# Attention B of a four-block transformer kernel: row maxima from four 32-row products at a time, the spread ahead of the second value block, the output copy behind the shift

## The reference

```
q = (x @ Wq.T).reshape(b, t, 8, 32)
kv_latent = x @ Wkv_down.T
k = (kv_latent @ Wk_up.T).reshape(b, t, 8, 32)
v = (kv_latent @ Wv_up.T).reshape(b, t, 8, 32)
scores = jnp.einsum('bqhd,bkhd->bhqk', q, k) * 32 ** -0.5
attn = jax.nn.softmax(scores, axis=-1)
out = jnp.einsum('bhqk,bkhd->bqhd', attn, v)
return out.reshape(b, t, 256) @ Wo.T
```

## Time and profile before

| | |
|---|---|
| median of three runs | 2250.07 us |
| the profiled execution's own time | 2249.5 us |
| its span | 2247.7 us |
| mean granted clock of TensorE | 0.981 of full speed |
| PE busy (share of the span) | 2099.7 us (93%) |
| DVE busy | 1919.2 us (85%) |
| ACT busy | 1734.8 us (77%) |
| POOL busy | 877.0 us (39%) |
| attention B's loop, first rate to last eviction | 1667.0 to 2116.2 us |

### The profile page before, as it was taken

How to read it: one execution, slowest core, us unless ns; L and a number is a source line. 1 busy time by engine, 2 the same in 40 slices (tenths; PEclk the granted TensorE clock), 3 DMA queues, 4 the chain that set the end, 5 groups by cost and what they waited for, 6 DMA issues and landing times. The chain is left out here.

```text
span 2247.7 us, 62135 instructions
## 1 busy us (share of the span) xinstructions
PE 2099.7 (93%) x24904; PEld 1428.6 (64%) x24904; DVE 1919.2 (85%) x2618; ACT 1734.8 (77%) x3070; POOL 877.0 (39%) x953
## 2 busy tenths in 40 slices
PE   6799999999999999999999999968779999999877
PEld 4467776777767777777777767754435656566644
DVE  6899999999999999999999999957678788887684
ACT  3789998999989999999999999942357777777532
POOL 4333323333223333333233233233017777777540
PEclk9999999999999999999999999988989999999988
DMA  3799999999999999999999999940141111111001
GB/s 102 119 197 195 195 196 185 195 193 193 193 194 197 194 197 195 191 197 189 198 194 191 194 192 194 197 83 1 35 137 31 30 31 33 34 32 35 9 1 38
DMA packets 1097040, 303.81 MB, mean 135 GB/s; under 512 B 1070256, under 2 KB 1090096, under 8 KB 1096496
## 3 DMA queue, kind: packets, MB, share of 16 engines
q1 hardware_dynamic: 1095888, 299.36, 76.5%
q10 hardware_dynamic: 864, 0.47, 0.1%
HBM read 20.83 MB, written 10.49 MB: 14 GB/s over the span
## 5 line engine op out<-in xcount | busy, mean ns | idle before, releaser
L453 DVE SCALAR_TENSOR_TENSOR a_parts<-a_probs,a_parts 128x1024 f16<-128x1024 f32 x512 | 659.1, 1287 | 79.4 <-ACT a_parts L405 78.7
L364 PE MATMUL a_out_ps<-a_vs,a_pT 128*128 128x128 f16 x4096 | 712.2, 219 | 4.7 <-DMA a_pT<-a_parts 4.6
L366 PE MATMUL a_out_ps<-a_vs,a_pT 128*128 128x128 f16 x4096 | 712.2, 219 | 0.0
L368 PE MATMUL a_out_ps<-a_vs,a_pT 128*128 128x128 f16 x4096 | 712.2, 219 | 0.0
L397 ACT ACTIVATE a_probs<-a_score_ps,a_negmax 128x1024 f32<-128x1024 f32 x512 | 571.4, 1116 | 94.1 <-DVE a_negmax L447 86.6
L447 DVE TENSOR_REDUCE a_negmax<-a_score_ps 128x1 f32<-128x1024 f32 x512 | 622.1, 1215 | 11.0 <-PE a_score_ps L350 7.2
L507 POOL TENSOR_TENSOR a_weighed<-a_own_out,wpost 128x256 f32<-128x256 f32 x256 | 247.1, 965 | 961.3 <-DVE a_parts L453 956.0
L405 ACT ACTIVATE a_parts<-a_probs 128x1024 f16<-128x1024 f32 x512 | 540.3, 1055 | 31.8 <-DMA a_pT<-a_parts 31.0
L364 PEld LDWEIGHTS a_out_ps<-a_vs,a_pT 128*128 128x128 f16 x4096 | 400.8, 98 | 64.8 <-ACT a_own_out L415 4.1
L366 PEld LDWEIGHTS a_out_ps<-a_vs,a_pT 128*128 128x128 f16 x4096 | 400.8, 98 | 59.5
L346 PE MATMUL a_score_ps<-kh,a_qs 128*128 128x512 f16 x1024 | 390.2, 381 | 42.3 <-ACT a_probs L397 34.9
(11 more groups left out here) (221 smaller groups left out, 2262.9 us busy)
## 6 DMA issues: line engine op xcount, KB each, us to landing
a_pT<-a_parts SPq DMA_TRANSPOSE x512, 5.0
b_qs<-q_parts SPq DMA_DIRECT2D x96, 64.0 KB, 1.9
b_ks<-k_parts SPq DMA_DIRECT2D x96, 64.0 KB, 1.9
q_parts<-b_parts SPq DMA_DIRECT2D x32, 128.0 KB, 1.9
k_parts<-b_parts SPq DMA_DIRECT2D x32, 128.0 KB, 1.9
x<-x_dram SPq DMA_DIRECT2D x4, 512.0 KB, 7.6
a_rope<-rope_dram SPq DMA_DIRECT2D x1, 2048.0 KB, 10.4
out_dram<-x SPq DMA_DIRECT2D x4, 512.0 KB, 5.4
```

The lines of the kernel that those rows point to most:

```text
L364: pe.matmul(out[:, 0:D], hi, vs[:, b, 0, j, :], start=j == 0, stop=False, skip_group_check=True)
L366: pe.matmul(out[:, 0:D], hi, vs[:, b, 1, j, :], start=False, stop=False, skip_group_check=True)
L368: last = pe.matmul(out[:, 0:D], lo, vs[:, b, 0, j, :], start=False, stop=j == JB - 1, skip_group_check=True)
L453: dve.scalar_tensor_tensor(out=parts[:, T % RING_P, 1, :], in0=probs[:, T % RING_P, :], scalar=PSCALE, in1=parts[:, T % RING_P, 0, :], op0 ...
```

## The change: what it does

- Two new tiles `b_q4` and `b_k4` hold the high parts of q and k four times over, once in each strip of 32 partitions. SP issues their eight DMAs of each head (64 KB each) ahead of the six there were, on semaphores of their own.
- `rate(g)` now makes two tiles of 128 queries at once: four matmuls of 32 rows by 512 columns, each on another strip of rows and into another of the four banks of `b_max_ps`. It uses the high parts alone. There are as many matmuls as before (8 to a unit). Group g waits until both maxima of group g - 1 are taken, so one group is in flight where there were two tiles.
- The PE's loop now is: scores 0 and 1, first value block, rate, scores 2 to 5, the next unit's spread, second value block, rate, scores 6 and 7. The rates run about two units ahead (`2u + 4`, `2u + 5`), one group further than before at the loop's start. Scores 0 of an even unit wait for the six older DMAs.
- ACT scales the next unit's maxima after exponential 3 (before: after 5), copies the shift after exponential 5, and then evicts (before: evicts first).
- DVE takes all four maxima of a unit and then inverts (before: three, inverts, one).

```
-            def rate(n):
-                u, t = n // TILES, n % TILES
...
-                if n >= 2:
-                    pe.wait_ge(max_ready, n - 1)
-                cols = slice(u % 2 * HALF + t * P, u % 2 * HALF + (t + 1) * P)
-                for c in range(2):
-                    last = pe.matmul(max_ps[n % 2][:, c * CH:(c + 1) * CH], qs[0:STACK, slot, cols],
-                                     ks[0:STACK, slot, c * CH:(c + 1) * CH], start=True, stop=True)
-                last.then_inc(rated, 1)
+            def rate(g):
+                u, half = g // 2, g % 2
...
+                if half == 0 and u % 2 == 0:
+                    pe.wait_ge(high_in[slot], 128 * (u // 2 // SLOTS + 1))
+                if g >= 1:
+                    pe.wait_ge(max_ready, 2 * g)
+                for k in range(2):
+                    at = u % 2 * HALF + (2 * half + k) * P
+                    for c in range(2):
+                        rows = slice((2 * k + c) * HDB, (2 * k + c + 1) * HDB)
+                        last = pe.matmul(max_ps[k][:, c * CH:(c + 1) * CH], q4[rows, slot, at:at + P],
+                                         k4[rows, slot, c * CH:(c + 1) * CH], start=True, stop=True)
+                    last.then_inc(rated, 1)
@@ sync
+                for r in range(TILES):
+                    rows = slice(r * HDB, (r + 1) * HDB)
+                    sp.dma_start(q4[rows, slot, :], q_dram[0, G]).then_inc(high_in[slot], 16)
+                    sp.dma_start(k4[rows, slot, :], k_dram[0, G]).then_inc(high_in[slot], 16)
@@ scores(u, 0)
+                    if u % 2 == 0:
+                        pe.wait_ge(qk_in[u // 2 % SLOTS], 96 * (u // 2 // SLOTS + 1))
@@ tensor
-            for n in range(TILES):
-                rate(n)
+            rate(0)
+            rate(1)
             pe.wait_ge(consts, 3)
             spread_max(0)
-            rate(TILES)
-            rate(TILES + 1)
+            rate(2)
+            rate(3)
             for u in range(units):
-                rate(TILES * (u + 1) + 2)
                 scores(u, 0)
                 scores(u, 1)
                 times_v(u - 1, 0)
-                rate(TILES * (u + 1) + 3)
+                rate(2 * u + 4)
                 scores(u, 2)
                 scores(u, 3)
-                rate(TILES * (u + 2))
                 scores(u, 4)
                 scores(u, 5)
+                spread_max(u + 1)
                 times_v(u - 1, 1)
-                spread_max(u + 1)
-                rate(TILES * (u + 2) + 1)
+                rate(2 * u + 5)
                 scores(u, 6)
                 scores(u, 7)
@@ scalar
-                for j in range(6):
+                for j in range(4):
                     exponentiate(u, j)
                 scale_max(u + 1)
+                exponentiate(u, 4)
+                exponentiate(u, 5)
+                keep_shift(u + 1)
                 evict(u - 1)
-                keep_shift(u + 1)
                 exponentiate(u, 6)
                 exponentiate(u, 7)
@@ vector
-            for n in range(TILES + 2):
+            for n in range(2 * TILES):
                 row_max(n)
             for u in range(units):
-                row_max(TILES * (u + 1) + 2)
-                row_max(TILES * (u + 1) + 3)
                 row_max(TILES * (u + 2))
+                row_max(TILES * (u + 2) + 1)
+                row_max(TILES * (u + 2) + 2)
+                row_max(TILES * (u + 2) + 3)
                 invert(u - 1)
-                row_max(TILES * (u + 2) + 1)
```

More of the change, by code:

```diff
@@ L552, in attend_b @@
         ks = st.sb(s, "b_ks", [P, SLOTS, SEQ], F16)
+        q4, k4 = st.sb(s, "b_q4", [P, SLOTS, SEQ], F16), st.sb(s, "b_k4", [P, SLOTS, SEQ], F16)
         ident16 = st.sb(s, "b_ident16", [P, P], F16)
@@ L564, in attend_b @@
         consts, qk_in = st.sem("b_consts"), [st.sem(f"b_qk_in{i}") for i in range(SLOTS)]
+        high_in = [st.sem(f"b_high_in{i}") for i in range(SLOTS)]
         rated, max_ready, nm_ready = st.sem("b_rated"), st.sem("b_max_ready"), st.sem("b_nm_ready")
@@ L597, in rate @@
                 slot = u // 2 % SLOTS
-                if t == 0 and u % 2 == 0:
-                    pe.wait_ge(qk_in[slot], 96 * (u // 2 // SLOTS + 1))
-                if n >= 2:
-                    pe.wait_ge(max_ready, n - 1)
-                cols = slice(u % 2 * HALF + t * P, u % 2 * HALF + (t + 1) * P)
-                for c in range(2):
-                    last = pe.matmul(max_ps[n % 2][:, c * CH:(c + 1) * CH], qs[0:STACK, slot, cols],
-                                     ks[0:STACK, slot, c * CH:(c + 1) * CH], start=True, stop=True)
-                last.then_inc(rated, 1)
+                if half == 0 and u % 2 == 0:
[9 more added lines that the diff above has]
+                    last.then_inc(rated, 1)
             def spread_max(u):
```

## The result

The changed kernel takes 2261.0 us (five runs, 2255.0 to 2264.7) against 2250.0 us: ratio 1.0047, interval 1.0032 to 1.0063. Timed a second time it came to 2261.5 against 2249.1, ratio 1.0058 (1.0041 to 1.0075). So it is 11 to 12 us slower, where 2260 was forecast.

The account below looks back on a forecast made before the run. PE's list bounds the kernel; after the change a PE-ACT chain of 6.96 us a unit would. Loop +7.0, start +1.8 and end +1.0 make +9.8 us, so 2260 us; 8-in-10 range 2246 to 2279.

Parts of the forecast that it names:

- PE's list was the bound: Attention B before the change: PE's own work sums to 6.78 of the 6.84 us a unit takes.
- The pack, r = 0.345: Four 32-row rate matmuls on PE, first start to next score: 0.03 + 0.215 + 0.10 = 0.345 us.
- The upper bounds of 0.50 and 0.96: Pack time in us if weights load one by one (0.50, rival 12%) or matmuls don't overlap (0.96, rival 4%).
- The chain, 6.27 + 2r = 6.96: PE and ACT waits through one unit of attention B, start to start: 6.96 us against 6.84 before.
- +7.0: Attention B's loop: 62 periods of 6.96 us less one pack, 431.2 us against 424.2.
- Spread ahead of the block: On PE, the second value block's 1.45 us no longer covers the scaling; the block now stands behind scaling and spread.
- Is each link the last to come?: Chain check: spread bound by scaling (1.22 us against 0.87), exponential 6 by scores 6 (2.22 against 2.00).
- the eviction's move brings nothing: On ACT, moving the eviction behind the shift copy brings nothing and costs nothing while 0.2 us of slack stands.
- DVE, POOL, SP hidden: Maxima rounds (2.89 us), POOL's 5.1 us a unit plus a division, and SP's 14 issues a head add no time.
- Start and end of the stage, +1.8 and +1.0: Attention B: unit 1's spread comes 1.8 us later; last spread to last eviction grows from 10.09 to 11.07 us.
- From stage to median: Stage change of +9.8 us added to the profiled 2249.5 us, then 0.6 for the median: 2259.9, rounded 2260.
- Rival 1: Attention B: PE's 5.85 us a unit decides and the chain doesn't bind, -59 us, 2191 us; 7%.

Follow-up runs that it names:

- experiment 1: Changed kernel with the spread behind the second value block again and ACT's list as before, packs and loads kept: 2250.4 us, ratio 1.0001.
- experiment 3: Changed kernel with each pack of four matmuls issued twice into the same banks: 2290.0 us, ratio 1.0168.
- experiment 2: Kernel before, with its 96-row rates, given only the new order: spread ahead of the second value block and ACT's new list: 2274.9 us, ratio 1.0105.
- experiment 7: Changed kernel with ACT scaling the next unit's maxima after exponential 1, not after exponential 3: 2254.8 us, ratio 1.0020.
- experiment 5: Kernel before, with the eight added loads of each head issued behind the six old ones and read by nobody: 2249.3 us, ratio 0.9999.
- Experiment 4: Changed kernel with PE's value blocks placed where PE would wait for ACT, ACT scaling after exponential 1 and evicting before the shift copy: 2217.0 us, ratio 0.9846.
- experiment 6: Kernel before, with its 96-row rates and loads, given the PE order and ACT list of Experiment 4: 2264.3 us, ratio 1.0069.
- experiment 9: Kernel of experiment 7 with the spread's wait for the scaling removed for u > 0, leaving the wait for exponential 3: 2255.1 us, ratio 1.0026.

## Why the prediction was right, point by point

- **PE's list was the bound, a chain through ACT stood close behind.** Confirmed: with 1.0 us of PE work a unit taken out and the order left, the period falls by 0.08 only, 0.11 in the steady loop (experiment 1).
- **The pack, r = 0.345.** It is 0.33 (1896.07 to 1896.40), 0.11 of it beyond one matmul's streaming. The term that was off is the start of the four, within 0.01 us and not 0.03. (The windows of the earlier trace rows count the matmuls running in them, two and then four in all, so what they show is four within 0.03.) The upper bounds of 0.50 and 0.96 fell with this reading and with the 0.22 of a doubled pack in experiment 3. The estimate from the Trainium skill ("TensorE: Matmul & The Clock Gate", Part 3: 3.07 times, so r = 0.38) was further off than the one from the rows.
- **The chain, 6.27 + 2r = 6.96.** The unit read above sums to the same with r = 0.33: 6.93, every link within 0.02 of its row of before. Of the 2 us between +7.0 and +5.0 the steady period explains 1.4 (6.94 for 6.96, by r), and the first period 0.5 (6.42), which the sum had put at the steady length.
- **Spread ahead of the block is the step that costs.** Experiments 1 and 2 confirm it for the spread together with ACT's list; the spread was not moved alone, so how the 0.37 us of experiment 2 divides between them is not shown.
- **Is each link the last to come?** Exponential 6 was bound by scores 6 with 0.25 idle on ACT before it, 0.22 forecast. But that the eviction's move brings nothing does not follow from this, and was wrong by the rows. With the old list the shift copy stands between the eviction and exponential 6, which then starts 1.00 us behind the eviction (1894.82 to 1895.82 in experiment 1, the same before). From the eviction at 1896.21 here that is 1897.21, where it started at 1896.83: by this estimate the move saved some 0.4 us a unit in this order. No run has the new order with the old list. A second detail was wrong: by scaling and spread 1.22 us against 0.87 by scores 5, I treated the scaling as the only late input. Exponential 3 itself, with two waits in front of the spread, was just as late (0.74); experiment 7 showed it.
- **DVE, POOL, SP hidden.** DVE idle 1.41 us a unit (1.4 forecast). The loads cost nothing (experiment 5).
- **Start and end of the stage, +1.8 and +1.0.** Measured +2.0 and +1.1. A slip inside: I took the load at 1663.74 for the first, and it was the third, since the window that I read began there; the first is at 1662.89. The step that used it, two issues of 0.46 more, was still right: first load to first pack went from 4.12 to 5.05 us.
- **From stage to median.** The forecast let the rest of the kernel stand. It didn't quite: 9.8 forecast and 8.1 found in the stage, but 11 to 12 in the median. Two errors of opposite sign bring the forecast within 1 us of the result, and that closeness is luck; by its own terms it was good to 2 or 3.
- **Rival 1 (faster, 2191).** Fell as long as this order stands. Experiment 4 shows what its condition was: PE must not wait for scaling and exponentials. There the period comes to 6.22 us, and one wait of PE a unit is still left; of 100 us in the steady window PE is busy 98, DVE and POOL 87 each.

## What to carry to other kernels

When an engine that is 100% busy gets less work, first write down the chain that runs through it and the engine behind it, start to start, and see what the removed work was covering; here 1.0 us of matmuls a unit was worth about 0.1 until the order was changed as well, and 0.6 with an order that suits. The order has to suit the work that is left: the same order with the old rates was slower than the kernel before (experiment 6). Put long independent blocks where an engine would wait for another's answer, and never behind an instruction that waits for a fresh one. Last instructions of a stage, where part of the work has run out, show such links at their bare length: all of those used here held in the middle of the loop too.

## What the runs showed of the hardware that I had not expected

A second semaphore wait ahead of a matmul cost 0.09 us (0.74 against 0.65, experiments 7 and 9), although that semaphore had been reached some 2 us earlier (in experiment 7 the scaling ends 2.1 us ahead of the spread). This is where PE stands still before the matmul. Where it streams, no cost shows: scores 0 of the changed kernel have one wait more in even units than in odd ones, and follow scores 7 after 0.22 us in both.

TensorE's clock differs between the kernels at the start of the stage, where PE mostly waits for loads and maxima. In the kernel before, the granted clock is 0.55 in the 18.6 us from first load to the spread of unit 1; in the changed one it is 0.50, the 1.2 GHz level, in all 20.65 us, in which PE is busy for 6.4. The forecast took most of its terms for the start from rows at that low clock, and came out 0.2 us short.

Behind the stage the clock differs between kernels whose code there is the same. The 20 us from the last eviction, in the kernel before, the changed kernel, and experiments 4 and 9 (window, its length, busy us by engine with counts, granted clock):

```profile
2115.83:2135.83 20.00, 14.57 (x512) 14.41 (x512) 14.91 (x73) 1.86 (x3) 0.46 (x1) 1.00 0.01 3
```

```profile
2127.09:2147.09 20.00, 16.20 (x512) 16.04 (x512) 13.35 (x59) 1.86 (x3) 0.45 (x1) 0.91 0.01 3
```

```profile
2082.97:2102.97 20.00, 16.14 (x512) 15.98 (x512) 13.41 (x60) 1.85 (x3) 0.45 (x1) 0.91 0.01 3
```

```profile
2113.76:2133.76 20.00, 14.91 (x512) 14.70 (x512) 14.67 (x71) 1.86 (x3) 0.45 (x1) 1.00 0.01 3
```

In this window PE runs the projection's 512 records and is idle otherwise. At a granted 1.00 (the 2.4 GHz level throughout) they take 14.57 us, in experiment 9 14.91; at a mean of 0.91, part of the window at 1.2 GHz, 16.1 to 16.2, so 1.6 us more. Of the eleven profiles, those of the kernel before, of the loads alone and of the covering order with 96-row rates show 14.57, experiment 9 shows 14.91, and the seven others 16.0 to 16.2, the changed kernel in both its profiles among them. In the 105 us after that the mean clock is between 0.85 and 0.90 from one profile to the next (0.90 before; 0.85 and 0.90 in the two of the changed kernel). The two together account for the time from the last eviction to the end: 131.9 and 132.1 us with 14.57 and 0.90, 133.3 to 133.6 with 16 and 0.90, 135.8 with 16.2 and 0.85. So the first is worth 1.6 us, the second about 2.2, and the 3.9 us behind the stage in the profiled pair are both.

Of the 3 to 4 us in the medians that the stage doesn't explain, 1.6 go with the projection, which ran at the lower clock in both profiles of the changed kernel; the rest stays open. All eleven executions of the changed kernel have a lower mean granted clock over the whole launch (0.975 to 0.980) than the kernel before has on average (0.981), which fits, but only the profiles say where. What decides the clock I didn't find: PE is idle for 2.3 us ahead of the projection in all eleven profiles, and no run was aimed at it.
